# A scan kernel's entry rearranged: shared gating, row copies and one batch's statistics change places

## What is computed

```python
x = x + 0.5 * ffn(layernorm(x))     # eight routed experts (top 1) and a shared one
x = x + attn(layernorm(x))          # the scan
x = x + 0.5 * ffn(layernorm(x))

# ffn, the shared expert
shared = silu(x @ shared_gate_w) * (x @ shared_up_w) @ shared_down_w

# attn, for 16 states n and 256 channels d
dt_x, Bm, Cm = split(x @ W_x.T, [64, 80])
dt = softplus(dt_x @ W_dt.T + b_dt)
dA = exp(dt[..., None] * -exp(A_log))
dBx = dt * Bm * x                   # an outer product over n
h = dA_t * h + dBx_t                # over 512 steps
y_t = sum_n(h * C_t);  y = y + x * D
```

## Time and profile before

| | us |
|---|---|
| runs: median (lowest to highest of 3) | 435.62 (433.93 to 435.76) |
| the profiled execution, device time | 438.39 |
| its span, first to last instruction | 436.70 |
| busy in the span: PE, DVE, ACT, POOL | 403.5, 327.0, 276.6, 267.4 |
| the transition, about | 110 to 144 |
| batch 0 of the scan: first recurrence to the first of batch 1 | 144.41 to 192.97 |
| last recurrence starts | 324.06 |

### The profile page before, as it was taken

The page is one execution under the profiler, slowest core; times in us unless marked ns, Lnnn a source line. Parts: engine busy times, 40 slices in busy tenths (PEclk is TensorE's granted clock), DMA queues, the critical chain, the costliest instruction groups (busy, mean ns, idle before and its releaser), DMA issues. The chain is left out here.

```text
span 436.7 us, 8333 instructions
## 1 busy us (share of the span) xinstructions
PE 403.5 (92%) x2716; PEld 280.8 (64%) x2716; DVE 327.0 (75%) x510; ACT 276.6 (63%) x516; POOL 267.4 (61%) x210
## 2 busy tenths in 40 slices
PE   5899899999977998999899999999999899899995
PEld 5436444444444978988898799888974556344452
DVE  4678555554287979999999999999897775456552
ACT  1431365655138789999999999998952210656552
POOL 6203446643329569888979798979881006577543
PEclk9899999999999799999999999999999999999999
DMA  8949214943424133864454448533310534344411
GB/s 251 386 153 284 59 44 136 306 155 134 152 68 97 53 96 119 145 124 151 134 111 109 144 133 144 134 117 119 124 50 0 192 99 116 93 120 136 120 52 49
DMA packets 50809, 56.85 MB, mean 130 GB/s; under 512 B 16327, under 2 KB 35596, under 8 KB 50768
## 3 DMA queue, kind: packets, MB, share of 16 engines
q1 hardware_dynamic: 46624, 45.78, 36.3%
q0 software_dynamic: 4144, 10.54, 8.1%
HBM read 41.14 MB, written 16.48 MB: 132 GB/s over the span
## 5 line engine op out<-in xcount | busy, mean ns | idle before, releaser
L526 POOL TENSOR_TENSOR gs<-hs,c_sb 128x1024 f32<-128x1024 f32 x63 | 148.2, 2373 | 26.2 <-PE bank L1057 17.4
L1426 DVE TENSOR_TENSOR_SCAN hs<-da,bank 128x1024 f32<-128x1024 f32 x64 | 143.9, 2273 | 3.7 <-PE bank L1033 1.9
L663 ACT ACTIVATE da<-dt_sb,a_neg 128x511 f32<-128x511 f32 x128 | 84.2, 709 | 1.6 <-DVE dt_sb L1389 1.2
L1057 PE MATMUL bank<-ident,gs 128*128 128x128 f32 x504 | 65.5, 273 | 2.0 <-POOL gs L526 2.0
L679 ACT ACTIVATE dbx_t<-dtx_t,h_sb 128x256 f32<-128x256 f32 x153 | 65.1, 495 | 0.8 <-DVE dtx_t L1395 0.7
L1057 PEld LDWEIGHTS bank<-ident,gs 128*128 128x128 f32 x504 | 56.7, 141 | 5.0 <-POOL gs L526 3.8
L882 PE MATMUL bank<-xnT,w_gu 128*128 128x512 f32 x112 | 51.6, 609 | 0.0
L1033 PE MATMUL bank<-ident,dbx_t 128*128 128x128 f32 x336 | 46.0, 282 | 5.1 <-DVE dbx_t L1410 1.8
L480 POOL DMA_INDIRECT da<-rows,row_token x29 | 30.1, 1038 | 30.4 <-issue 30.1
L1033 PEld LDWEIGHTS bank<-ident,dbx_t 128*128 128x128 f32 x336 | 39.0, 145 | 8.7 <-issue 5.3
L591 ACT ACTIVATE th<-bank,da 128x256 f32<-128x256 f32 x36 | 17.1, 474 | 43.0 <-PE bank L921 30.4
(11 more groups left out here) (184 smaller groups left out, 772.3 us busy)
## 6 DMA issues: line engine op xcount, KB each, us to landing
c_sb<-c_dram SPq DMA_DIRECT2D x64, 256.0 KB, 3.5
rows<-xn_no SPq DMA_DIRECT2D x8, 516.0 KB, 5.3
diag_dram<-dbx_t SPq DMA_DIRECT2D x6, 512.0 KB
routing<-diag_dram SPq DMA_DIRECT2D x11, 256.0 KB, 3.5
slot_m<-diag_dram SPq DMA_DIRECT2D x11, 256.0 KB, 3.5
rows<-xn_no SPq DMA_DIRECT2D x1, 2064.0 KB, 9.1
x_sb<-in_x SPq DMA_DIRECT2D x4, 512.0 KB, 6.7
w_gu<-in_gate_w SPq DMA_DIRECT2D x2, 1024.0 KB, 10.0
```

What stands on the lines that cost most here:

```text
L526: nc.gpsimd.tensor_tensor(gs[:, s % 2], hs[:, s % RING], c_sb[:, s % RING].unsqueeze(1).to_broadcast([P, KC, L]), ALU.mult).then_inc(sc_g, 1)
L663: nc.scalar.activation(da[:, s % RING, k, 1:L], dt_sb[:, k, seq(s // N)][:, 1:L], ACT.Exp, scale=a_neg[:, k, s % N:s % N + 1]).then_inc(sc ...
L1057: mm = nc.tensor.matmul(YA[k][:, i * P:(i + 1) * P], products[:, k, i * P:(i + 1) * P], ident[:], start=(s % N == 0 and i == 0), stop=(s % ...
L1426: nc.vector.tensor_tensor_scan(hs[:, s % RING].rearrange(flat), da[:, s % RING].rearrange(flat), DBX[s % 2][:, :, :].rearrange(flat), 0.0, ...
```

## The change

1. The second half of batch 3's shared gating, (0, 3, 1), uses the banks H and Silu instead of YS and Tanh; its hidden step on DVE is then one operation instead of two. DVE takes hidden(0, 3, 0) right behind hidden(0, 2, 1), ahead of normalise(1, 0), and hidden(0, 3, 1) ahead of `project_dtx`.
2. dt of batch 0 is turned into YS instead of YA. `shared_down(0, 3)` therefore waits for `project_dt` and no longer for `project_dtx`; its halves stand ahead of `turn_dbx(0)` and behind `turn_dbx(1)`, and its results on DVE in slots 0 and 1 instead of 1 and 2.
3. PE's `warm` has 6 products instead of 9, into YS. Pairs 3, 4 and 5 are turned earlier, and ACT copies pairs 2 and 3 ahead of the first decay, 4 and 5 behind the next two states.
4. DVE takes two rows of state 3's outer product instead of one.
5. The statistics of batch 3 (DVE), its factor and shift (POOL) move from slot 5 to slot 10 of batch 0; ACT normalises in slots 12 to 15 instead of 9 to 12.

```diff
@@ -49,7 +49,7 @@
     RING = 4
     TURNS = 3
     STATES = BATCH * N
-    BY_DVE = ((2, 2, 2, 1, 1, 1) + (0,) * 10,) + ((1, 1, 0, 1) + (0,) * 12,) * 2 + ((0,) * 16,)
+    BY_DVE = ((2, 2, 2, 2, 1, 1) + (0,) * 10,) + ((1, 1, 0, 1) + (0,) * 12,) * 2 + ((0,) * 16,)
     DIAG = ((6, 7, 9, 10, 12, 14),) + ((4, 6, 7, 9, 11, 13),) * 2 + ((3, 6, 9, 12),)
     BLOCKS = 6
     DIAGS = 2
@@ -248,11 +248,11 @@
 
         def shared_banks(r, b, fo):
 
-            return (H[0], H[1]) if fo == 0 else (YS[0], YS[1]) if r == 1 or b in (0, 3) else (T, Y)
+            return (H[0], H[1]) if fo == 0 or (r, b) == (0, 3) else (YS[0], YS[1]) if r == 1 or b == 0 else (T, Y)
 
         def by_silu(r, b, fo):
 
-            return (r, b, fo) not in ((0, 0, 0), (0, 3, 1)) and (r, b) not in ((1, 0), (1, 1))
+            return (r, b, fo) != (0, 0, 0) and (r, b) not in ((1, 0), (1, 1))
 
         def by_tanh(u):
 
@@ -527,7 +527,7 @@
                                             ALU.mult).then_inc(sc_g, 1)
                     if b == 0 and n == 3:
                         combine(BATCH - 1)
-                    if b == 0 and n == 5:
+                    if b == 0 and n == 10:
                         rstd_of(1, BATCH - 1)
                         shift(1, BATCH - 1)
                     if b > 0 and n == 3:
@@ -708,10 +708,8 @@
                         ahead(N * b + n + AHEAD)
                     if not more and n - 1 in PIECES:
                         tanh_piece(PIECES.index(n - 1))
-                    if b < 2 and n == 0:
-                        ln_copy(1, 5 + b)
-                    if b == 1 and n == 1:
-                        ln_copy(1, 7)
+                    if b == 1 and n < 2:
+                        ln_copy(1, 6 + n)
                     if (b, n) in ((0, 1), (2, 0)):
                         project_copy(b + 1)
                     late = (2, 1, 0, 0)[b]
@@ -726,8 +724,8 @@
                         project_copy(2)
                     if b > 0 and 6 <= n < 6 + LT:
                         normalise(2, b - 1, n - 6)
-                    if b == 0 and 9 <= n < 9 + LT:
-                        normalise(1, BATCH - 1, n - 9)
+                    if b == 0 and 12 <= n < 12 + LT:
+                        normalise(1, BATCH - 1, n - 12)
                     turn = 13 if more else 10
                     if b > 0 and n in (turn, turn + 1):
                         ln_copy(2, 2 * (b - 1) + n - turn)
@@ -758,14 +756,15 @@
             project_ln(0)
             shared_gate(0, 3, 1)
             nc.scalar.preload_act_table_set(EXP_LN)
+            for q in (2, 3):
+                ln_copy(1, q)
             act.wait_ge(a_ready, 2)
             act.wait_ge(pj_dt, KC)
             decay(0)
             outer(0)
             for s in range(1, AHEAD):
-                ln_copy(1, 1 + s)
                 ahead(s)
-            ln_copy(1, 4)
+                ln_copy(1, 3 + s)
             for b in range(BATCH):
                 scan(b)
             for fo in range(KC):
@@ -850,7 +849,7 @@
                 if (r, b) == (0, 2):
                     pe.wait_ge(ff_yc, NR)
                 if (r, b) == (0, 3):
-                    pe.wait_ge(pj_dtx, 2)
+                    pe.wait_ge(pj_dt, KC)
                 elif (r, b) == (1, 0):
                     pe.wait_ge(sc_x, KC * BATCH)
                 for q in (2 * b + h for h in halves):
@@ -867,7 +866,7 @@
                 if (r, b, fo) == (0, 1, 1):
                     pe.wait_ge(rt_read, 1)
                 if (r, b, fo) == (0, 3, 1):
-                    pe.wait_ge(sh_x, 6)
+                    pe.wait_ge(sh_hidden, 7)
                 elif (r, b) == (1, 1):
                     pe.wait_ge(sc_h, STATES - 1 + fo)
                 elif b > 0 and (r, b, fo) != (0, 1, 1):
@@ -1010,7 +1009,9 @@
                 pe.wait_ge(pj_dt, KC * (b + 1))
                 if b > 0 and h > 0:
                     pe.wait_ge(pj_dtx, 2 * b + h)
-                dst = YA[h] if b == 0 else T
+                if b == 0:
+                    pe.wait_ge(sh_x, 6)
+                dst = YS[h] if b == 0 else T
                 for i in range(2):
                     for k in range(KC):
                         lo = (b % 2) * L + (2 * h + i) * P
@@ -1022,9 +1023,9 @@
                 if s >= 2:
                     pe.wait_ge(sc_h, s - 1)
                 elif s == 0:
-                    pe.wait_ge(sh_hidden, 7)
+                    pe.wait_ge(sh_hidden, 8)
                 else:
-                    pe.wait_ge(sh_hidden, 8)
+                    pe.wait_ge(pj_dtx, 2)
                 if s in PLAIN:
                     pe.wait_ge(sc_act, states_by("act", s + 1))
                     pe.wait_ge(sc_dve, states_by("dve", s + 1))
@@ -1076,9 +1077,6 @@
                         add(s - 1)
                     if s + 2 < STATES:
                         turn_dbx(s + 2)
-                    if s == 0:
-                        shared_down(0, 3, (1,))
-                        ln_transposes(1, 5)
                     if last_one(s):
                         shared_gate_up(1, 1, 0, (0,))
                     if s == 1:
@@ -1135,15 +1133,17 @@
             project_bt(0)
             shared_gate_up(0, 3, 1)
             ln_transposes(1, 2)
-            pe.wait_ge(sh_hidden, 7)
-            warm(H[0], 9)
+            pe.wait_ge(sh_x, 6)
+            warm(YS[0], 6)
+            ln_transposes(1, 3)
             for h in range(2):
                 turn_dt(0, h)
+            shared_down(0, 3, (0,))
             turn_dbx(0)
-            ln_transposes(1, 3)
+            ln_transposes(1, 4)
             turn_dbx(1)
-            ln_transposes(1, 4)
-            shared_down(0, 3, (0,))
+            shared_down(0, 3, (1,))
+            ln_transposes(1, 5)
             for b in range(BATCH):
                 scan(b)
             add(STATES - 1)
@@ -1391,7 +1391,7 @@
             def project_dtx(b, h):
 
                 dve.wait_ge(pj_tp, 2 * b + h + 1)
-                src = (YA[h] if b == 0 else T).rearrange("p (i d) -> p i d", i=2)
+                src = (YS[h] if b == 0 else T).rearrange("p (i d) -> p i d", i=2)
                 nc.vector.tensor_tensor(dtx_t[:, b % 2, 2 * h:2 * h + 2, :], src, xn[:, LT * b + 2 * h:LT * b + 2 * h + 2, :],
                                         ALU.mult).then_inc(pj_dtx, 1)
 
@@ -1425,9 +1425,9 @@
                     flat = "p k t -> p (k t)"
                     nc.vector.tensor_tensor_scan(hs[:, s % RING].rearrange(flat), da[:, s % RING].rearrange(flat),
                                                  DBX[s % 2][:, :, :].rearrange(flat), 0.0, ALU.mult, ALU.add).then_inc(sc_h, 1)
-                    if b == 0 and n in (1, 2):
-                        shared_result(0, 3, (n - 1,))
-                    if b == 0 and n == 5:
+                    if b == 0 and n in (0, 1):
+                        shared_result(0, 3, (n,))
+                    if b == 0 and n == 10:
                         dve.wait_ge(back_x, BATCH)
                         stats_of(1, BATCH - 1)
                     if b > 0 and n == 1:
@@ -1485,6 +1485,7 @@
             dve.wait_ge(back_x, 1)
             stats_of(1, 0)
             shared_hidden(0, 2, 1)
+            shared_hidden(0, 3, 0)
             normalise(1, 0)
             combine(1)
             dve.wait_ge(back_x, 2)
@@ -1494,15 +1495,14 @@
             dve.wait_ge(back_x, 3)
             stats_of(1, 2)
             project_bt(0)
-            shared_hidden(0, 3, 0)
             for k in range(KC):
                 project_w(0, k)
             for k in range(KC):
                 project_dt(0, k)
+            shared_hidden(0, 3, 1)
             for h in range(2):
                 project_dtx(0, h)
             outer(0)
-            shared_hidden(0, 3, 1)
             outer(1)
             for b in range(BATCH):
                 scan(b)
```

## The result

| | before | after |
|---|---|---|
| median, us | 435.62 (433.67 to 437.64, 11 runs) | 437.83 (436.61 to 438.84, 11 runs) |
| ratio after/before | | 1.0055 [1.0035, 1.0076] |
| profiled execution, us | 438.39, span 436.70 | 438.01, span 436.3 |
| mean granted clock of the profiled execution | 0.986 | 0.993 |

The medians say 2.2 us slower, and the two profiled executions say 0.4 us faster. The forecast was 436.2, range 433.1 to 438.5.

A forecast was written before the change was run, and what follows sets the result against it. DVE, with its 64 scans almost without waiting, was taken to bound the kernel. 2.52 us early, less 1.74, less 1.47, plus 0.11 made 0.6 late: median 436.2, range 433.1 to 438.5.

The forecast's parts named there:

- The hidden steps: DVE, shared gating of batch 3: both moved operations, 0.69 us each, fit idle times of 0.95 and 0.75; cost nothing.
- the statistics: DVE, slot 10 of batch 0: among back-to-back scans they cost 1.74 us; bounds 0 to 2.27.
- POOL's four operations: POOL, behind its product 10: 1.95 us of small operations, ending near 182.0, hidden by over 2 us.
- The normalisations: ACT, slots 12 to 15: three behind its dtx wait add 1.47 us; 0.69 late there, 0.58 comes through.
- DVE's wait for project_ln of batch 2: DVE, end of batch 1: this wait of 0.82 us, until 213.30, would end at 213.9 and exceed 2 us.
- ACT's pause for PE: ACT, before project_ln of batch 2: its 0.62 us pause at 205.40 would be gone.
- the wait for dtx: ACT, second dtx of batch 1: its wait, until 187.94 before, would end near 187.2, 0.78 us early.
- 2.52 for the entry: Transition into batch 0's scans: with PE at full clock and the new order, project(1) starts at 150.85, 2.52 us early.
- sign of being wrong: Either a clock of 0.50 after 138, or batch 1's slot 7 scan starting earlier than its old 214.64.
- 1 (ACT absorbs): ACT's 0.69 us lateness vanishes in its pause at 205.40, DVE's 0.78 gain stays: 434.8; chance 0.17.
- 2 (the gain is kept whole): Another engine than DVE paces slots 10 to 16, hiding both moved works: 2.5 us gained, 433.1; chance 0.11.
- rival 3: PE's clock falls between 137.4 and 148 all the same: 2.3 us of gain lost, 2.9 late, 438.5; chance 0.14.

The follow-up runs named there:

- the entry alone: The changed kernel with batch 3's statistics and shift put back to slot 5 and its normalisations to slots 9 to 12; 433.95 us, ratio 0.9982.
- before, again: The kernel before, unchanged, measured again with the granted clock of each execution; 434.96 us, ratio 1.0014.
- the run without warm-up: The kernel before without PE's 9 useless products ahead of the transposes of dt; 436.78 us, ratio 1.0044.
- after, again: The changed kernel, unchanged, measured again with the granted clock of each execution; 438.22 us, ratio 1.0064.
- normalise late: The changed kernel with batch 3's statistics and shift back in slot 5, normalisations left in slots 12 to 15; 436.19 us, ratio 1.0029.
- the statistics alone: The kernel before with only batch 3's statistics and shift moved to slot 10 and its normalisations to slots 12 to 15; 438.49 us, ratio 1.0092.

## Why the prediction came out as it did

*The steps.* On the execution that it was worked out on, nearly every step came true. The hidden steps fit into DVE's holes. Between dt and project(1) the forecast had 12.40 (150.85 less 138.45); 12.58 was measured. DVE waits for project_ln in any case (0.85 until 166.74), so the statistics were free at slot 5: the entry alone has them there and reaches scan 8 at 30.71, after at 30.70. At slot 10 they cost 1.70, forecast 1.74. POOL's four operations behind them held up nothing: from scan 11 to scan 16 it is 12.94 before and after.

*The normalisations* cost 1.48 from scan 16 on, where the working had 1.47 less 0.11. The price was right, the place was not: I let it arrive at DVE's wait for project_ln of batch 2, which was to grow beyond 2 us, and that stayed 0.82. ACT's lateness reaches DVE earlier, through PE: the last transposes of batch 3 now wait 1.06 for ACT's copy, PE has no hole from there to the transposes for scan 21 (205.35), and scan 21 waits 0.80. Then L1375 waits 0.54 for ACT itself. The prediction had PE's wait and followed it to ACT's pause, but not to the scan that stands in between. ACT's pause for PE, which was to disappear, is still 0.62 long:

```profile
197.74 0.63 PE L809 MATMUL bank<-ident,xn_no 128*128 128x128 f32 x4 [1.06 <-ACT xnT L562]
```

```profile
183.40 0.59 ACT L686 ACTIVATE xn_no<-x_sb,mean_rstd,rstd 128x256 f32<-128x256 f32 x1
...
186.18 1.31 ACT L679 ACTIVATE dbx_t<-dtx_t,h_sb 128x256 f32<-128x256 f32 x3 [0.97 <-DVE dtx_t L1395]
187.39 0.59 ACT L686 ACTIVATE xn_no<-x_sb,mean_rstd,rstd 128x256 f32<-128x256 f32 x1
...
205.11 0.69 ACT L636 ACTIVATE w_exp<-bank,b_sb 128x512 f32<-128x512 f32 x1 [0.62 <-PE bank L1005]
```

The first is a row of PE's timeline of after. Those of ACT's answer: one normalisation ahead of the wait for dtx, the next behind it. That wait ends at 186.18, 48.80 behind the addition; 187.2, as forecast, would have been 48.75.

*The step that failed* is a sentence of the first part: "I work out a difference and put it on both", the profiled execution and the median. The largest term, 2.52 for the entry, was the difference to an execution in which the clock had fallen. Of its size as measured between the first two profiles (2.40 at scan 8), 2.15 is what the fall cost at that point (33.10 against 30.95), and 0.24 is what the new order brings (30.95 to 30.71). With 0.2 in place of 2.4, the sum is 1.70 + 1.48 - 0.19, 2.99 late; the trace shows 2.93, and the two comparisons of medians +2.2 and +3.3 (1.0064 of 434.96 gives 2.8). The warning stood beside it: the profiled execution was 2.77 above the median. I read that as a constant offset, but the price of the fall was in it: of the 3.57 by which the first profile is longer than that of before, again (438.39 against 434.82), 2.25 lie behind the addition, and 1.32 ahead of it, although the kernel is the same.

One sign of being wrong did show: the scan of slot 7 of batch 1 starts at 214.35, ahead of its old 214.64. That says nothing of the change, since this execution reaches the addition 1.07 sooner; counted from there the scan is 0.78 late.

*The rivals.* 1 (ACT absorbs) and 2 (the gain is kept whole) fell with the rows of scan 11 and of scan 21. 3 gave 438.5, close to what came, but by a mechanism that isn't there: the clock of after is 1.00 throughout the transition. Its arithmetic, both payments and next to no gain from the entry, holds when the clock falls in neither kernel as well as when it falls in both. The time alone would have seemed to confirm it; the row of the stretch refutes it. That 437.83 lies between 433.1 and 438.5 is luck: the upper end was rival 3's price, and the forecast itself is 1.6 off.

In the run without warm-up PE does nothing but transposes from 132.85 to 144.54, and within this time the clock not only falls but comes back to 1.00, by 144.4. The rule weighed for rival 3 is that of the Trainium skill, "TensorE: Matmul & The Clock Gate", Part 4 (PE-mode transpose): a transpose doesn't count as a busy PE in the same way for the clock. The trace of this run doesn't agree with it: transposes alone stood ahead of the rise.

*A fall ahead of the addition.* In before, again and in after, again the clock falls at the same place, 130 to 134, and the products of the shared gating take 5.40 instead of 3.70. It costs the new order 0.77 at project(1) (after, again; normalise late) and the old one nothing. ACT's and PE's rows of after, again, then ACT's first decay in before, again:

```profile
135.43 0.60 ACT L574 ACTIVATE hs<-bank 128x512 f32<-128x512 f32 x1 [0.77 <-PE bank L881]
138.08 0.63 PE L809 MATMUL bank<-ident,xn_no 128*128 128x128 f32 x4 [0.91 <-ACT xnT L562]
```

```profile
137.92 1.34 ACT L663 ACTIVATE da<-dt_sb,a_neg 128x511 f32<-128x511 f32 x2 [0.46 <-DVE dt_sb L1389]
```

In both orders ACT waits for these products and is 0.77 late. In the old one it has a wait for dt behind them, 1.23 in the statistics alone, which shrinks to 0.46, and nothing is lost. In the new one ACT copies pair 2 at that place and PE turns pair 3 ahead of dt, so pair 3 (1.07 behind the addition, not 0.30), dt (1.53, not 0.77) and project(1) are all 0.77 late. With this fall in both, the new order is not 0.24 ahead at scan 8 but 0.54 behind (31.49 against 30.95).

*Open:* what decides, in an execution of the old order, whether the clock falls behind the addition. The first profile and that of the statistics alone have the same work and the same idle times of PE there, and only one has the fall. The Trainium skill, "TensorE: Matmul & The Clock Gate", Part 1 (The HAM clock gate), names a cause that would fit: the window in which the chip looks at PE runs freely, so its phase to the program differs from run to run. The trace agrees as far as the place of the fall differs between executions of one kernel (141.3, 130.3); no run here shows the phase as such.

## What to carry to other kernels

Before pricing an edit, set the profiled execution against the median: where they differ by as much as the gain in question, look for what this execution has that others lack (here one stretch in the clock column), and price the edit both with it and without. Work moved to a slot where its engine runs back to back cost its full length here, and work moved behind the only wait of its engine lost that cover; both could be read from the timeline to within 0.1 us. A late engine hits the first consumer that has no slack, which here was not the one that waited longest. A wait taken out of the old order may have been the cover for something that happens in some executions only.

## What the runs showed of the hardware that was not expected

- The same program has a granted clock of 0.50 for 6.8 us behind the addition in one profile and 1.00 in another, with PE idle for 1.04 and 1.83 us ahead in the one and for 1.05 and 1.83 us in the other (before, statistics only). The mean clock of 20 of 90 executions of before is below 0.988, with a median of 436.95 against 434.40.
- What PE does ahead of the stretch seems to move this: where it idles for 3.15 and 1.78 us, all 10 executions have a mean clock of 0.989 or less, and with two added warm-ups all 12 have 0.992 or more; in the new order 4 of 70 are below 0.988, and none of its six profiles has a fall between 136 and 150. Useless products on PE cost nothing at the end (295.95 against 295.97).
- With transposes alone on PE from 132.85 to 144.54, the clock fell to 0.50 at 137.5 and was back at 1.00 by 144.4 (no warm-up).
- A stretch at half clock can cost 2.25 us at the end (141.3 to 148.1) or nothing behind it (130.3 to 133.7 in before, again, where ACT's wait for dt took it up); the same fall at 130 costs the new order 0.77, where this wait is gone.
